# Bias products of the first expert layers: four 32-row tiles replaced by 64-row tiles on two masked copies

## What is computed

```python
x = x + attn(cond(x, itok_B_0_15, ...), ...)           # conditional linear layer, then 16-head attention
t = lora(x, language_ids) + lang_embed[language_ids]    # 4 languages, rank 16
ys = geglu(t @ Ws1 + bs1) @ Ws2 + bs2                   # shared expert, 2 * 512 hidden columns
h  = t @ We1[e] + be1[e]                                # 12 experts, 2 * 768 hidden columns
yr = sum over the top 2 experts of w * (geglu(h) @ We2[e] + be2[e])
out = x + ys + yr
```

## Time and profile before

| | |
|---|---|
| median of 3 runs | 955.81 us (953.32 to 957.62) |
| profiled execution | 958.14 us, of which the span from first to last instruction 956.2 us |
| mean granted TensorE clock | 0.978 of full speed |
| TensorE matmul busy | 920.3 us (96%) |
| VectorE, ScalarE, GpSimd busy | 516.2, 295.6, 402.4 us |

### The profile page before, as it was taken

One profiled execution on the slowest core, in us unless ns is written; L12 is line 12 of the kernel. 1 busy time (PEld: TensorE's weight loads), 2 busy tenths in 40 slices (PEclk: granted clock), 3 DMA queues, 4 the chain that ended last, 5 costly groups with the idle time before them and its releaser, 6 DMA issues.

```text
span 956.2 us, 28042 instructions
## 1 busy us (share of the span) xinstructions
PE 920.3 (96%) x9693; PEld 698.1 (73%) x9694; DVE 516.2 (54%) x1154; ACT 295.6 (31%) x783; POOL 402.4 (42%) x511
## 2 busy tenths in 40 slices
PE   7889999999999999899999899999999999999995
PEld 6667777777777777656666677777777777777774
DVE  2575555555555566556775245555454555545452
ACT  0333333333333333243232223232332323233230
POOL 2133333333333332100000366666666666666652
PEclk8999999999999999889999799999999999999998
DMA  8434445545454432015742122222222222222221
GB/s 269 114 98 151 151 151 151 151 151 151 151 151 151 151 86 79 1 51 176 220 171 63 68 30 35 31 30 34 28 35 28 34 30 31 33 28 35 28 32 23
DMA packets 49005, 85.60 MB, mean 90 GB/s; under 512 B 7267, under 2 KB 27555, under 8 KB 48835
## 3 DMA queue, kind: packets, MB, share of 16 engines
q1 hardware_dynamic: 33634, 68.76, 23.1%
q0 software_dynamic: 13888, 15.13, 11.9%
q10 hardware_dynamic: 1440, 1.16, 0.5%
HBM read 68.48 MB, written 16.55 MB: 89 GB/s over the span
## 4 chain that ended last, share of the span: by engine, by line
PE 93%; DVE 3%; ACT 1%; issue 1%; DMA 1%; ACTq 1%; DVEq 0%; POOL 0%
PE ps L1380 21%; PE ps L1368 15%; PE ps L1106 7%; PE ps L1284 6%; PE ps L1273 4%; PE ps L1363 4%; PE ps L1201 4%; PE ps L1159 4%; PE ps L1117 4%; PE ps L1085 3%; PE ps L1147 3%; PE ps L1175 3%; PE ps L1205 2%; PE ps L1187 2%; PE ps L1352 2%; PE ps L1139 2%
## 5 line engine op out<-in xcount | busy, mean ns | idle before, releaser
L1380 PE MATMUL ps<-arena,stage 128*128 x900 | 208.5, 382 | 0.0
L1380 PEld LDWEIGHTS ps<-arena,stage 128*128 128x128 f32 x900 | 166.7, 192 | 20.0
L470 POOL DMA_INDIRECT out_dram<-stage,to_row x75 | 120.6, 1608 | 129.0 <-DVE stage L1015 126.1
L1368 PE MATMUL ps<-token_rows,token_rows_T 64*128 64x128 f32 x1800 | 163.6, 301 | 0.0
L627 ACT ACTIVATE stage<-ps 128x384 f32<-128x384 f32 x150 | 65.5, 488 | 281.9 <-PE ps L1368 281.9
L1368 PEld LDWEIGHTS ps<-token_rows,token_rows_T 64*128 64x128 f32 x1800 | 119.9, 189 | 15.2
L995 DVE COPY token_rows<-ps 128x128 f32<-128x128 f32 x75 | 21.9, 291 | 169.3 <-PE ps L1353 169.3
L462 POOL DMA_INDIRECT token_rows<-gated_rows,from_row x75 | 75.0, 1000 | 87.6 <-DVE to_row L907 64.9
L386 POOL TENSOR_TENSOR arena<-arena 128x256 f32<-128x256 f32 x32 | 23.2, 726 | 195.9 <-DVE arena L749 195.9
L1106 PE MATMUL ps<-arena 128*128 128x128 f32 x512 | 75.8, 292 | 5.4 <-ACT arena L523 5.4
L1000 DVE TENSOR_TENSOR stage<-ps,stage 128x384 f32<-128x384 f32 x150 | 75.9, 548 | 2.3 <-ACT stage L627 2.3
(11 more groups left out here) (169 smaller groups left out, 1437.2 us busy)
## 6 DMA issues: line engine op xcount, KB each, us to landing
stage<-in_we_dram SPq DMA_DIRECT2D x36, 512.0 KB, 4.5
arena<-in_cond_w_dram SPq DMA_DIRECT2D x64, 256.0 KB, 2.8
arena<-in_we_dram SPq DMA_DIRECT2D x12, 768.0 KB, 4.3
arena<-in_x_both_dram SPq DMA_DIRECT2D x32, 256.0 KB, 2.6
arena<-in_L_cond_bias_dram SPq DMA_DIRECT2D x64, 64.0 KB, 2.7
out_dram<-arena SPq DMA_DIRECT2D x32, 128.0 KB, 1.7
be_bc<-in_be_rows_dram SPq DMA_DIRECT2D x13, 192.0 KB, 2.7
gated_rows<-token_rows POOLq DMA_DIRECT2D x2, 1152.0 KB, 10.1
```

The costliest lines, as they stand in the source:

```text
L470: pool.indirect_dma_start(out_rows, bass.IndirectOffsetOnAxis(to_row[:, t:t + 1], 0), y_sb[t % YR], None, compute_op=ALU.add).then_inc(d_a ...
L1368: last = mm(ps[:, 2 * g + hf, at], w1x[s % 2][64 * g:64 * g + 64, j * CW + hf * P:j * CW + (hf + 1) * P], s_rowT[s % 2][64 * g:64 * g + 64 ...
L1380: last = mm(ps[:, 4 + s % 2, 0:D], actT_sb[s % 2][:, hf, j * P:(j + 1) * P], arena[:, ds(e * E2 + (NJ * hf + j) * D, D)], start=(hf == 0 a ...
```

## The change

The bias products no longer run on four groups of 32 rows but on two groups of 64. A group of 64 partitions holds the bias rows of the two quarters `hf` = 0 and `hf` = 1. To pick one of them, the language rows (the moving operand) exist in two copies, each multiplied by a new constant column `half` that is 1 on the 32 rows of its quarter and 0 on the others. The numbers of bias products, weight loads and fp32 products stay as they are.

```diff
@@ constants and tensors
-                  in_tile=P, part_back=1, pad_row=1, id_high=2 * PAIRS)
+                  in_tile=P, part_back=1, pad_row=1, id_high=2 * PAIRS, half=2)
-        langB = sb("lang_rows", [P, B], bf16)
+        langB = sb("lang_rows", [P, 2, B], bf16)
-        sh_lang = sb("unit_lang", [P, 2, U // S], bf16)
+        sh_lang = sb("unit_lang", [P, 2, 2, U // S], bf16)
-        s_langT = [cut(P // 2).bitcast(bf16) for _ in range(2)]
+        s_langT = [[cut(P // 2).bitcast(bf16) for _ in range(2)] for _ in range(2)]
@@ ScalarE, unit_copy
-                copy(sh_lang[:, half, :], langB[:, ds(u * (U // S), U // S)]).then_inc(shx_ok, 1)
+                copy(sh_lang[:, half, :, :], langB[:, :, ds(u * (U // S), U // S)]).then_inc(shx_ok, 1)
@@ VectorE, start
-            V.tensor_scalar(langB[:, :], lang_tmp, col["lang_row"], col["one_row"], ALU.is_equal, ALU.add)
+            link(V.tensor_scalar(lang_tmp, lang_tmp, col["lang_row"], col["one_row"], ALU.is_equal, ALU.add))
+            for hf in range(2):
+                V.tensor_scalar(langB[:, hf, :], lang_tmp, col["half"][:, hf:hf + 1], None, ALU.mult)
@@ VectorE, rowT_copy
-                V.tensor_copy(s_langT[s % 2], ps[:, 7, P:2 * P]).then_inc(rowT_sb, 1)
+                for hf in range(2):
+                    last = V.tensor_scalar(s_langT[s % 2][hf], ps[:, 7, P:2 * P], col["half"][:, hf:hf + 1], None, ALU.mult)
+                last.then_inc(rowT_sb, 1)
@@ TensorE, hidden
-                           w1b[32 * r:32 * r + 32, unit * P:(unit + 1) * P],
-                           sh_lang[32 * r:32 * r + 32, half, :].unsqueeze(2).to_broadcast([32, U // S, S]),
+                           w1b[64 * g:64 * g + 64, unit * P:(unit + 1) * P],
+                           sh_lang[64 * g:64 * g + 64, half, hf, :].unsqueeze(2).to_broadcast([64, U // S, S]),
                            start=True, stop=False)
@@ TensorE, first_layer
-                    for r in range(4):
-                        mm(ps[:, r, at], w1bx[s % 2].bitcast(bf16)[32 * r:32 * r + 32, at],
-                           s_langT[s % 2][32 * r:32 * r + 32, :], start=True, stop=False)
+                    for hf in range(2):
+                        for g in range(2):
+                            mm(ps[:, 2 * g + hf, at], w1bx[s % 2].bitcast(bf16)[64 * g:64 * g + 64, at],
+                               s_langT[s % 2][hf][64 * g:64 * g + 64, :], start=True, stop=False)
@@ shape_constants
+        "half": (p[:, None] % 64 // 32 == np.arange(2)),
```

## The result

The changed kernel takes 903.63 us (median of 4 runs, 901.47 to 904.39) against 956.71 us for the kernel before beside it (4 runs, 953.32 to 957.98). The ratio is 0.9447, 95% interval 0.9415 to 0.9478: 53.1 us less. The forecast was 906.5 us, range 898 to 922. The profiled execution took 904.39 us with a span of 902.5 us; that of before 958.14 and 956.2 us.

A forecast was written before the change was run, and what follows sets the result against it. TensorE was taken to bound both stages. Savings of 33.8 us (routed), 14.3 and 2.0 (shared), less 0.6 lost, make 49.5; from 958.14 profiled this gives 908.6, as a median 906.5 us predicted, range 898 to 922.

The forecast's parts named there:

- The bound: Shared and routed stages: TensorE sets the time, so a nanosecond off its sequence is a nanosecond off the kernel.
- Units 0 to 2: Shared units before the choice of experts: 2 us saved, bounds 0 and 3.3; part turns into a longer wait.
- Routed blocks, inner: Routed stage, between blocks of a tile: 0.28 us in place of 0.47, 0.195 saved, bounds 0.165 and 0.20.
- the gap belongs to the change of the row split: Around bias products: the pauses come from switching 64 to 32 rows and back, not from the number format.
- First block of a tile: Routed stage: only the inner switch goes, 0.20 us in place of 0.26; 0.06 saved, between 0.02 and 0.10.
- Shared blocks: Shared stage: 0.54 us a block for 0.85, 0.305 saved per inner block, 1.10 a unit; 14.3 us in units 3 to 15.
- What was added: VectorE's extra masked copy, 0.21 us per tile, is covered inside the routed stage; 0.6 us lost in all.
- idle stretches that grow at the borders: Sign against the forecast: it is wrong if the idle stretches at the borders grow; no size given.
- A: Rival: in a row-split array, weights of another format cannot load under same-row matmuls; 20 us saved, 935.5 us; chance 0.08.
- B: Rival: the gap is not the row switch, drains stay and a second round is added; 969 us; chance 0.05.
- C: Rival: VectorE or GpSimd holds the routed tile at about 5.2 us, 19 us back, 925 us; chance 0.05.
- main case: Prediction's own account: TensorE saves the row switches in both stages; own range 901 to 920 us; chance 0.82.

The follow-up runs named there:

- e4: Changed kernel, but block 1 alone of the routed first layer has its bias products on 32 rows; 916.6 us, ratio 0.9574, routed tile 5.10 us.
- e5: Changed kernel, but the routed first layer issues all three blocks' bias products first, on 32 rows, then all fp32 products; 893.4 us, ratio 0.9339.
- e1: Changed kernel, but the shared expert's bias products take 32-row slices again, routed stage on 64 rows; 919.3 us, ratio 0.9596.
- e2: Changed kernel, but the routed bias products take 32-row slices again, shared stage on 64 rows; 940.1 us, ratio 0.9818.
- e3: Changed kernel, but both kinds of bias products on 32-row slices of the masked copies, keeping VectorE's added work; 958.6 us, ratio 1.0007.
- e8: Changed kernel with two more mask operations per routed tile on VectorE, into a spare tensor; 903.2 us, ratio 0.9431.
- e10: e5 with a single unmasked copy of the language rows, as in the kernel before; 892.9 us, ratio 0.9351 to the kernel before.
- e9: Changed kernel with four more mask operations per routed tile on VectorE, into a spare tensor; 934.0 us, ratio 0.9782, routed tile 5.32 us.
- e6: Changed kernel, but all three blocks' routed bias products come first, on 64 rows, then all fp32 products; 892.8 us, ratio 0.9327.

## Why the prediction was right

**The bound** was read rightly: TensorE in both stages. In the routed stage the saved steps came through one to one: from the transposes to the next tile's first bias product both kernels take 2.96 us (median), so the whole 0.495 us by which the tile shrinks lies in the three blocks. Units 3 to 15 give what their blocks give. Units 0 to 2 do not, as foreseen: part of their saving becomes the longer wait of `ranks()`.

**Routed blocks, inner.** Forecast 0.195 us. From bias product to bias product 0.190 and 0.200 are saved, and 0.104 from the last block's bias product to the transposes (medians of the tiles), 0.495 in all. Less the 0.09 of the first block, below, the two inner gaps gave 0.20 each. The step "the gap belongs to the change of the row split" is what e4 and e5 show: put back in one block, it costs at both borders; taken out of the 32-row layout, it is gone. The Trainium skill says under "TensorEngine Tiling (Array Packing)", "Key Properties", that a change of tiling mode drains the array while a change of tile does not. The trace agrees. In the kernel before, 0.10 us pass between the fp32 columns and the bias products; behind them the fp32 weights start to load 0.16 us after the bias round starts, 0.10 more than the round's 0.057, and this load (0.10) lies bare. In the changed kernel, where all of these products are on 64 rows, neither pause is there, and none is at the format changes of the earlier trace rows.

**First block of a tile.** Forecast 0.06, measured 0.09: the bias round starts 0.004 us after the start of its weight load (median), where the forecast took 0.03 that no row gave. Per tile 0.495 in place of 0.45; 75 tiles give 37.1 in place of 33.8 us. This is the largest error of the sum.

**Shared blocks.** Forecast 0.305 and 1.10 us a unit; measured 0.30 (0.846 to 0.543) and 1.11. Units 3 to 15: 14.4 us (14.3 forecast). No engine held them up: the masks for the row numbers were ready in time. Units 0 to 2 gave 3.0 us in the profiles where 2 was taken, and the wait of `ranks()` for VectorE grew from 0.23 to 1.83 us, as the text said it would for the last six blocks. But about half of the 3.0 us is the granted clock and not the change. Between 399 and 413 us it is 0.63 on average where it was 0.51 before: the stretch at 1.2 GHz there lasts 10.2 us, before 13.7. Profiles with the same clock in these units separate the two. From the first bias product to `ranks()` the kernel before takes 19.46 us and e5, with the shared stage of the change, 17.80, with the first 5.9 and 5.2 us of it at 1.2 GHz. e1, on 32 rows, takes 16.85 and e2, on 64, 15.35, both at 2.4 GHz throughout. So the change is worth about 1.5 us in these units, and the 2 us taken were a little too much. The sum had no term for the clock.

**Start of the routed stage.** From the first routed bias product to the end 38.4 us were saved, 1.3 more than the 37.1 of the tiles. The clock is the likely cause: the stage starts with two stretches of 3.4 us at 1.2 GHz where there was one of 13.7, and its first two tiles take 5.72 and 6.50 us, before 5.97 and 9.15. In the twelve profiles of this case, what the stage takes beyond its 75 tile periods is 13.1 to 13.8 us with 3.4 us at 1.2 GHz at its start, 15.4 to 16.3 with 6.8 or 10.2 us, and 16.0 to 16.6 with 13.7. No run set the clock on purpose.

**What was added.** The price of a second mask was mis-sized, without consequence. Two masks take VectorE 652.64 − 652.13 = 0.51 us, the one copy before took 0.20, so 0.31 more in place of 0.21. Inside the stage they were covered all the same: e3 measures it, and e8 even with another 0.52. Where the prediction saw no cover, at the stage's first tile and at the next tile's multiplications, the waits of TensorE grew from 1.77 to 2.05 and from 1.63 to 1.94 us, 0.6 in all where twice 0.21 was forecast. e8, with two more masks, has 2.57 and 2.46 there, e10, with none, 1.72 and 1.63. The prediction allowed 0.6 us lost in all, the start of the kernel included. The attention stage's end lies 0.8 us later in the profile (406.89 against 406.13). In the eleven profiles with this attention stage the same mark lies anywhere between 403.6 and 408.8 us, so a price of the added start work can't be read from it.

**The border.** The 1.3 us lost between the shared and the routed stage stood in no term but for 0.3, the masks of the first tile, forecast with 0.21. The other 1.0 is a sum on VectorE (L933) that starts 1.0 us after the end of the shared expert's last matmul, where it follows at once in the kernel before. It is not bound to the change: from the start of that last matmul to the first transpose there are 1.1 us in the kernel before, and with the shared stage of the change 2.1 in the changed kernel, e9 and e10, 1.3 and 1.2 in e2 and e4, and 1.1 in e5 to e8. What delays it in some executions stays open. The prediction named idle stretches that grow at the borders as a sign of being wrong, and they did grow: at `ranks()`, which its own sum had foreseen, and here. Together with the masks that is about 3 us, beside 53 saved, so the sign was drawn too sharply.

**The rivals.** A (no weight load beneath a matmul of the same rows across formats) is refuted by the row at 654.80. The Trainium skill's sentence that it leaned on ("TensorE: Matmul & The Clock Gate", Part 3, "What overlaps and what doesn't") is contradicted by this trace also for unequal formats. A grain of it is true in another way: the fp32 load is longer than a bf16 round, 0.05 us of it stays bare per block, and e6 takes most of that back. B (the gap is not the row switch) falls with the result, and its underlying worry, that four side by side is the better packing, is half right: e5 with 32 rows is as fast as e6 with 64. The fault of the kernel before was to switch to it three times a tile. C (another engine) falls: VectorE had 0.67 us left, GpSimd 1.2 us. In the chances, main case, A and C add up to 0.95, not to the 0.94 given for faster.

## What to carry to other kernels

Price a matmul that uses another row split than its neighbours by its two borders, not by its own record: here about 0.3 us per visit for 0.06 us of work. Either give it the neighbours' split, even if that needs twice the rounds, or do all such products in one visit. In the routed stage the second way needed no masks and no second copy: e10, with the shared stage of the change, lies 62.7 us under the kernel before in its set, where the change lies 53.1 under it. Distances between starts show this; busy time points the other way.

## What the runs showed of the hardware

- The change of row split, in numbers: 0.10 us from the end of the streaming to the next weight load, and the weight load that follows (0.10 for fp32) cannot lie under it. It is paid at each change: in e4 the block before the 32-row one grows by 0.10 us (64 to 32), and the 32-row block by 0.10 net of the bf16 round of 0.056 that it saves (32 to 64, with the bare fp32 load).
- A change of format at the same split adds no pause, on 128 rows and on 64 (weights at 654.80, 654.96). What stays bare is the part of a load that the round above it is too short to cover: 0.05 us of an fp32 load under a bf16 round of 0.056.
- VectorE's copy of 128 × 256 fp32 within SBUF (L265) takes 0.28 us where no copy of GpSimd runs beside it (all 87 such copies in the routed stages of the twelve profiles, 0.280 to 0.285) and up to 0.98 where one or two do. That the overlap is the cause is read from this, no run took GpSimd's copies away. The groups say it with means: routed stage of the changed kernel, then of e9, whose VectorE comes later.

```profile
L265 DVE COPY token_rows_T<-w_merged 128x256 f32 x72 | 54.1, 752 | 0.2
```

```profile
L266 DVE COPY token_rows_T<-w_merged 128x256 f32 x64 | 18.1, 283 | 0.0
```

  752 ns against 283 for the same copy: before, it was 634. The rows at 653.46 to 653.80 above show the overlap. It hid in VectorE's idle time in every kernel here.
